# Two-block kernel: second-layer weights, W_out, Wqkv and a fourth weight pair loaded in 32-wide blocks and turned by VectorE

## What is computed

```
xn = layernorm(x)
s0 = xn + rmsnorm(kvec * (xn @ W_in.T) @ W_out.T) * norm_w     # recurrent step from a zero state
ffn = fwht(silu(xn @ W1.T) * (xn @ W3.T)) @ W2.T                # H = 1024
x  = x + s0 * silu(ffn)
xn = layernorm(x);  z = layernorm(xn) * gamma + beta
s1 = softmax(causal(z Wq (z Wk).T / 16)) @ (z Wv) @ Wo + xn
x  = x + s1 * silu(ffn with the second layer's weights)
```

## Time and profile before

| | |
|---|---|
| median of 3 runs | 363.26 us (363.02 to 363.34) |
| profiled execution | 363.3 us, its span 361.5 us |
| PE, PEld, DVE, ACT, POOL busy | 98%, 83%, 69%, 47%, 28% |
| DMA | 38.63 MB in 42336 packets, 34.8% of 16 engines on SP's queue |
| chain that ended last | PE 94%, DMA 3%, DVE 1%, SP queue 1% |

### The profile page before, as it was taken

The page is one execution under the profiler, slowest core; times in us unless marked ns, Lnnn a source line. Parts: engine busy times, 40 slices in busy tenths (PEclk is TensorE's granted clock), DMA queues, the critical chain, the costliest instruction groups (busy, mean ns, idle before and its releaser), DMA issues.

```text
span 361.5 us, 5052 instructions
## 1 busy us (share of the span) xinstructions
PE 355.8 (98%) x1821; PEld 301.5 (83%) x1821; DVE 250.6 (69%) x481; ACT 169.2 (47%) x335; POOL 100.8 (28%) x126
## 2 busy tenths in 40 slices
PE   7999999999999999999999999999999999999996
PEld 4878888888888888888988878888888888888896
DVE  5669965886489647868568894788646887356645
ACT  2865371355135623554275544644446354454510
POOL 2154410246014723467506030060300603004000
PEclk9999999999999999999999999999999999999999
DMA  7995110525145623440242401424204332054001
GB/s 239 287 320 198 60 59 0 176 58 170 35 133 159 190 74 117 120 145 0 72 134 67 141 0 60 151 54 126 81 30 160 74 117 88 0 190 111 20 3 58
DMA packets 42336, 38.63 MB, mean 107 GB/s; under 512 B 5700, under 2 KB 41800, under 8 KB 42312
## 3 DMA queue, kind: packets, MB, share of 16 engines
q1 hardware_dynamic: 42168, 38.25, 34.8%
q10 hardware_dynamic: 144, 0.07, 0.1%
HBM read 24.09 MB, written 14.22 MB: 106 GB/s over the span
## 4 chain that ended last, share of the span: by engine, by line
PE 94%; DMA 3%; DVE 1%; SPq 1%; issue 0%; ACT 0%
PE GU L362 19%; PE GU L363 19%; PE GU L364 19%; PE O L362 8%; PE O L363 8%; PE O L364 8%; DMA stage<-in_L_ffn_W 3%; PE O L369 1%; PE T L369 1%; PE O L433 1%; PE T L362 1%; PE T L364 1%; PE T L363 1%; PE O L519 1%; PE O L518 1%; PE O L517 1%
## 5 line engine op out<-in xcount | busy, mean ns | idle before, releaser
L730 ACT ACTIVATE hf<-GU 128x512 f32<-128x512 f32 x64 | 38.2, 599 | 80.3 <-DVE hid L854 55.8
L1001 DVE TENSOR_TENSOR hf<-hf,GU 128x512 f32<-128x512 f32 x64 | 43.6, 681 | 32.5 <-PE GU L364 27.1
L362 PE MATMUL GU<-XT,W1T 128*128 128x512 f32 x128 | 50.8, 397 | 0.0
L364 PE MATMUL GU<-XT,W1T 128*128 128x512 f32 x128 | 49.9, 390 | 0.0
L363 PE MATMUL GU<-XT,W1T 128*128 128x512 f32 x128 | 49.9, 390 | 0.0
L362 PE MATMUL GU<-XT,W3T 128*128 128x512 f32 x128 | 49.9, 390 | 0.0
L364 PE MATMUL GU<-XT,W3T 128*128 128x512 f32 x128 | 49.8, 389 | 0.0
L363 PE MATMUL GU<-XT,W3T 128*128 128x512 f32 x128 | 49.8, 389 | 0.0
L854 DVE TENSOR_TENSOR hid<-hf,hid 128x512 fp32r<-128x512 f32 x64 | 48.2, 754 | 1.2 <-ACT hid L661 0.8
L362 PE MATMUL O<-hid,W2hi 128*128 128x512 f32 x112 | 44.0, 393 | 0.0
L363 PE MATMUL O<-hid,W2hi 128*128 128x512 f32 x112 | 43.7, 390 | 0.0
(11 more groups left out here) (204 smaller groups left out, 741.2 us busy)
## 6 DMA issues: line engine op xcount, KB each, us to landing
stage<-in_L_ffn_W SPq DMA_DIRECT2D x24, 256.0 KB, 5.6
swap_rows<-GX SPq DMA_DIRECT2D x7, 512.0 KB, 3.6
sT<-swap_rows SPq DMA_DIRECT2D x28, 128.0 KB, 2.7
swap_gate<-GX SPq DMA_DIRECT2D x7, 512.0 KB, 2.9
sT<-swap_gate SPq DMA_DIRECT2D x28, 128.0 KB, 2.7
swap_p<-PX SPq DMA_DIRECT2D x4, 640.0 KB, 3.2
PL<-swap_p SPq DMA_DIRECT2D x16, 160.0 KB, 3.2
swap_w<-GX SPq DMA_DIRECT2D x4, 512.0 KB, 2.9
```

Source lines behind the costliest of these rows:

```text
L362: pe.matmul(o, lhs(0), rhs(0), start=start, stop=False)
L364: return pe.matmul(o, lhs(1), rhs(0), start=False, stop=stop)
L730: act.activation(hf[:, c % 2, :], GU[:, c % 2, 0, :], ACT.Silu).then_inc(silu_done, 1)
L1001: dve.tensor_tensor(hf[:, c % 2, :], hf[:, c % 2, :], GU[:, c % 2, 1, :], ALU.mult).then_inc(mul_done, 1)
```

## The change

Weights that TensorE transposed, or that went over DRAM, are now loaded so that only 32 x 32 blocks are left to turn. `load_blocks` issues four DMAs a matrix; each fills 32 partitions, and each contiguous run that it reads is 32 floats. VectorE turns the blocks in place (`in_place`).

- First layer's fourth pair: W1 and W3 by blocks (8 DMAs), turned by VectorE in front of `nat_lo(3)`, hi by ACT, lo by POOL (`last_hi`, `last_lo`); chunk 6 waits for `last_lo`. W2 as before.
- W_out and Wqkv: by blocks (4 DMAs each) right into `woutT` and `wqkvT`; turned by VectorE (`turn_wout` after chunk 5, `turn_wqkv` after chunk 6).
- Second layer: W1 and W3 by blocks into `stage` (8 DMAs a pair), W2 by blocks into U2 (4 DMAs for all). VectorE turns them in groups 1 and 2, ACT makes hi, POOL makes lo. No `swap_w`, no transposes on TensorE past the head; a Hadamard product behind chunk 7 in groups 1 and 2, and behind chunk 1 in groups 2 and 3.
- The scaling of win by kvec goes from VectorE to ACT. `normalise(1)` comes ahead of `k_vector` and chunk 5.
- X is loaded in three parts; its last 1 MB comes behind Wqkv and Wo.
- All butterflies of the second layer are in groups 2 and 3.

```diff
+            def load_blocks(to, src, done):
+
+                blocks = src.rearrange("(d b) (c q a) -> q b c d a", b=Q, q=QUADS, a=Q)
+                for q in range(QUADS):
+                    sp.dma_start(to[q * Q:(q + 1) * Q].rearrange("b (c d a) -> b c d a", d=D // Q, a=Q), blocks[q]).then_inc(done, 16)
...
-            sp.dma_start(X[:, TILES:, :], xt_dram[:, TILES:, :]).then_inc(xrest_loaded, 16)
+            sp.dma_start(X[:, TILES:2 * TILES, :], xt_dram[:, TILES:2 * TILES, :]).then_inc(xnext_loaded, 16)
...
-            sp.dma_start(wout[:, :, :], W_out.rearrange("(a p) n -> p a n", p=P)).then_inc(small_loaded, 16)
+            load_blocks(woutT[:, :, :].rearrange("p m d -> p (m d)"), W_out, wout_loaded)
             sp.wait_ge(w2_tr, 2)
-            load_pair(0, 3, stage[:, 1, :, :], stage_loaded[1])
+            for w, m in enumerate((W1[0], W3[0])):
+                load_blocks(stage[:, 1, w, :], m[6 * P:8 * P, :], stage_loaded[1][w])
...
-            load_pair(1, 0, stage[:, 0, :, :], stage_loaded[0])
-            sp.wait_ge(w2_tr, PAIRS)
-            load_pair(1, 1, stage[:, 1, :, :], stage_loaded[1])
+            load_w(PAIRS)
             move_rows(1)
+            sp.wait_ge(last_lo, 2)
+            load_w(PAIRS + 1)
+            load_blocks(U2[1][:, :, :].rearrange("p c d -> p (c d)"), W2[1], w2_loaded)
             for n in range(1, NB):
                 move_gate(n - 1)
-                for j in ((0,), (1, 2), (3,))[n - 1]:
-                    move_w(PAIRS + j)
+                if n == 2:
+                    load_w(PAIRS + 3)
                 if n == NB - 1:
                     spread_c2(0)
                 move_rows(n + 1)
-                if n < 3:
-                    sp.wait_ge(w1_lo, 2 * KC * n)
-                    sp.wait_ge(w2_tr, PAIRS + n)
-                    load_pair(1, n + 1, stage[:, (n + 1) % 2, :, :], stage_loaded[(n + 1) % 2])
+                if n == 1:
+                    load_w(PAIRS + 2)
...
@@ TensorE: head and groups
-                head_pair(3)
                 head_pair_w2(3)
...
             def small_m():
-                pe.wait_ge(kstep, KSTEPS)
-                pe.wait_ge(sm_nat, 2)
+                pe.wait_ge(win_scaled, MC)
+                pe.wait_ge(wout_turned, MC // 2)
...
             def block0_group(n):
-                pe.wait_ge(u_ready, PAIRS + (0, 2, 3)[n - 1])
+                pe.wait_ge(u_ready, PAIRS + (0, 1, 3)[n - 1])
...
+                    if c == 1 and n > 1:
                         pe.wait_ge(gateT_ready, 2 * n)
-                        next_pair_w2(PAIRS + (0, 2, 3)[n - 1])
...
+                        next_hadamard(PAIRS + 2 * n - 3)
+                if n < 3:
+                    pe.wait_ge(gateT_ready, 2 * n)
+                    next_hadamard(PAIRS + 2 * n - 2)
                 recurrent_mix(n)
...
@@ VectorE: the head
-                dve.wait_ge(xrest_loaded, 16)
-                pair_lo(0, 3, 3)
+                dve.wait_ge(xnext_loaded, 16)
+                for w in (0, 1):
+                    dve.wait_ge(stage_loaded[1][w], 80)
+                    in_place(stage[:, 1, w, :]).then_inc(last_turned, 1)
                 nat_lo(3, w2nat)
                 stats(1, TILES)
                 chunk(0, 4)
+                normalise(1, TILES)
                 k_vector()
                 chunk(0, 5)
-                normalise(1, TILES)
+                turn_wout()
                 x_turn(1)
                 chunk(0, 6)
+                turn_wqkv()
                 w2_sums(0)
...
@@ POOL: groups 1 to 3
+                if n > 1:
+                    nat_lo(PAIRS + 2 * n - 3)
+                    pair_butterfly(1, 2 * n - 4, PAIRS + 2 * n - 3)
...
+                pool.wait_ge(xn_ready, n + 3)
+                if n < 3:
+                    pair_lo(PAIRS + 2 * n - 2)
+                    nat_lo(PAIRS + 2 * n - 2)
+                if n > 1:
+                    pair_butterfly(1, 2 * n - 3, PAIRS + 2 * n - 2)
+                    quad_butterfly(1, n - 2, (17, 23)[n - 2])
+                if n < 3:
+                    pair_lo(PAIRS + 2 * n - 1)
+                else:
+                    last_butterfly(1, 25)
```

More of the change, by code:

```diff
@@ L164, in two_block_kernel, with landed @@
         xT = [[XT[:, a, k, :] for k in range(KC)] for a in (0, 1)]
[L165 to L177, removed]
+        def landed(i):
+            return (32, 80)[i % 2] + 64 * (i // 2 - 1)
         def blocks_of(a, c0, c1):
@@ L279, in move_p @@
                                  swap_p[j].rearrange("(q a) f -> a q f", q=QUADS)).then_inc(p_moved, 16)
[L281 to L289, removed]
             def spread_c2(m):
@@ L435, in small_m @@
                 last.then_inc(sm_mm, 1)
[L436 to L439, removed]
             def small_av():
-                pe.wait_ge(sm_nat, 5)
+                pe.wait_ge(wqkv_turned, 3)
+                pe.wait_ge(wo_loaded, 16)
                 for i in range(KC):
@@ L467, in up_chunk @@
                     pe.wait_ge(xt_ready, 2 * n + 2)
-                if first and c % 2 == 0:
+                if first and c in (2, 4):
                     pe.wait_ge(w_lo, c + 2)
+                elif first and c == 6:
+                    pe.wait_ge(last_lo, 2)
                 if c >= 2:
@@ L667, in pair_hi, with turned_hi, turned_nat_hi @@
                        w_tr, 2 * i + w + 1, w_hi)
-            def landed_hi(i):
-                act.wait_ge(w_moved, 64 * (i - PAIRS) + 64)
-                for w in (0, 1):
-                    for k in range(KC):
-                        act.activation(w_part(0, i, w, k), w_landed(i, w, k), ACT.Copy).then_inc(w1_hi, 1)
+            def turned_hi(i):
+                cols = bass.ds(2 * P * (i - PAIRS), 2 * P)
+                for w, WT in enumerate((W1T[1], W3T[1])):
+                    hi(WT[:, 0, :, cols], stage[:, i % 2, w, :].rearrange("p (k h) -> p k h", k=KC), w_turned, 2 * (i - PAIRS) + w + 1, wx_hi)
+            def turned_nat_hi(i):
+                j = i - PAIRS
+                act.wait_ge(h_done, i)
+                hi(w2nat[:, 0, :, :], U2[1][:, 2 * j:2 * j + 2, :], w2_turned, j + 1, natx_hi)
             def pair_u(l, i, j):
@@ L759, in block0_head @@
                 pair_u(0, 2, 2)
-                pair_hi(0, 3, 3)
+                for w, WT in enumerate((W1T[0], W3T[0])):
+                    hi(WT[:, 0, :, 6 * P:8 * P], stage[:, 1, w, :].rearrange("p (k h) -> p k h", k=KC), last_turned, w + 1, last_hi)
                 nat_hi(3, w2nat)
@@ L764, in block0_head @@
                 pair_u(0, 3, 3)
-                small_hi([(woutT[:, 2 * h:2 * h + 2, :].rearrange("p a d -> p (a d)"), T[:, h, :]) for h in (0, 1)],
-                         2, sm_tr, 1, sm_nat)
                 hi(gb[:, :, :].rearrange("p g k -> p (g k)"), O[:, 0, 0:2 * KC], gb_tr, 1, gb_ready)
+                act.wait_ge(kvec_ready, 1)
+                for m in range(MC):
+                    act.activation(win[:, m, :], win[:, m, :], ACT.Identity, scale=kvec[:, m:m + 1]).then_inc(win_scaled, 1)
                 chunk(0, 6, True)
                 hi(flat[0], O[:, 0, :], sm_mm, 1, sm_hi)
-                small_hi([(wqkvT[:, w, :, :].rearrange("p a d -> p (a d)"), (T[:, 0, :], T[:, 1, :], O[:, 1, :])[w]) for w in range(3)],
-                         3, sm_tr, 3, sm_nat)
                 w2_hi(0)
@@ L888, in k_vector @@
                 dve.tensor_reduce(kvec[:, :], kprod[:, 0, :, :], AX_X, ALU.add).then_inc(kvec_ready, 1)
-                dve.wait_ge(kvec_ready, 1)
-                for m in range(MC):
-                    dve.tensor_scalar(win[:, m, :], win[:, m, :], kvec[:, m:m + 1], None, ALU.mult).then_inc(kstep, 1)
             def small_lo(q):
```

142 lines of the change are left out of this document (73 added, 69 removed).

## The result

| | before | after |
|---|---|---|
| median | 363.26 us | 366.91 us (366.80 to 367.21, 5 runs) |
| profiled execution, its span | 363.3, 361.5 us | 367.18, 365.4 us |
| ratio to before, 95% interval | | 1.0105 (1.0094 to 1.0116) |

The change costs 3.65 us. I had forecast 360.9, a gain, with 364.5 as the upper end of the range: wrong in sign, and outside the range.

What follows compares the result with a forecast made beforehand. TensorE, busy 98%, was taken as the bound. Gains of 0.72 us (head) and 1.76 us (groups 1 to 3), 2.5 us off 363.3, gave 360.8, forecast as 360.9; its own range 360.2 to 361.8, the full range 359.5 to 364.5.

Steps and rivals of the forecast that it cites:

- Step (1) of the head: Chunk 4 on TensorE, with 4 transposes instead of 12 ahead, starts at 25.0 instead of 26.48 us.
- DMA step: SP's queue: W_out and fourth-pair blocks, at 1030 packets in a us, take 8.0 us, through at 24.5; W3 needed at 25.9.
- third rival: Fourth pair's blocks land late, VectorE waits before its turn; slower than before from 2.5 us late, about 720 packets/us; chance 0.18.
- The rival of the clock: TensorE's clock falls at the new 3.1 us stall ahead of M, which takes up to 3.45 us more; chance 0.10.
- Steps (2) to (4): Head: chunk 6 at 31.05; VectorE's list stalls TensorE 3.1 us, M at 37.05; head ends at 49.66, winning 0.72 us.
- the meeting: Rival: VectorE's normalisation in the head runs beside POOL's butterflies, costing 1.1 us for one tile, 4.5 for four; chance 0.14.
- fourth rival: The rival of the clock: clock drop from 2.4 to 1.2 GHz behind the stall ahead of M, 362.6 to 364.3; chance 0.10.
- By 0.5 us an operation it is done 0.2 us before: Group ends: ACT finishes the second pair 0.2 us before the U copy is needed; otherwise a few tenths in two groups.
- Moving the last butterflies forward costs nothing on TensorE: Second layer: moving its last butterflies forward adds no TensorE time.
- the price of the transposes: TensorE: 0.11 us each, 44 removed, 4.8 us: 3.08 in the head and 1.76 in groups 1 to 3.
- no wait for the turned Wqkv: Head: VectorE's three turns of Wqkv end near 41.2 us, needed at 43.4, so hidden.
- no wait for POOL's late Hadamard input: Group 1: POOL's W2 subtraction ends at 82.2, TensorE wants it after chunk 7 at 83.2; one us to spare, no stall.

Runs made afterwards that it cites:

- k12_fill: Changed kernel with 18 unused 512-column matmuls on TensorE ahead of its wait for W2 of the fourth pair; 364.76 us, 1.0041 of the kernel before.
- k4_pairfirst: Changed kernel with the fourth pair's W2, then its W1 and W3 blocks, loaded ahead of W_out's blocks; 366.37 us, 1.0087 of the kernel before.
- k9_warm: k4_pairfirst plus 15 unused 512-column matmuls on TensorE ahead of the waits of product M; 363.03 us, 0.9993 of the kernel before.
- k8_runs: Changed kernel, W_out and the fourth pair's W1 and W3 read as contiguous runs, same DMAs and bytes, output differs; 365.81 us, 1.0067 of before.
- k7_best: Changed kernel with fourth pair loaded and transposed as before, ACT's U copy first, c2 turned a chunk earlier; 361.05 us, 0.9936 of before.
- k2_ucopy: Changed kernel with ACT's copy of U ahead of the second pair's high halves in groups 1 and 2; 365.44 us, 1.0062 of before.
- k3_c2: Changed kernel with the small turn of c2 one chunk earlier in group 3; 365.64 us, 1.0066 of the kernel before.
- k11_all: k7_best with chunk 7 ahead of the product M on TensorE; 359.83 us, 0.9908 of the kernel before.
- k5_oldpair: Changed kernel with the fourth pair loaded (3 DMAs) and transposed on TensorE as before; 362.26 us, 0.9968 of the kernel before.
- k1_w2first: Changed kernel with W2 of the fourth pair issued ahead of that pair's block loads; 368.32 us, 1.0139 of the kernel before.

## Why the prediction was wrong, point by point

The sum was 360.8 for the profiled execution, and that took 367.18. By stretches: the head +3.57 (53.23 against 49.66), groups 1 to 3 +1.38 (-0.38 instead of -1.76), group 4 +1.45 (nothing forecast): 6.40.

- **Step (1) of the head failed: "chunk 4 starts at 25.0".** It started at 29.75. My own DMA step had W3 through at 24.5, with W2 behind it in the queue; I named that and gave it 0.3 us. W2 landed at 29.1, and TensorE stood for 4.6 us. TensorE needs W2 at 24.5, before it needs W1 or W3, so the deadline of "W3 needed at 25.9, fits by a us" was the wrong one to test.
- **The DMA step was mis-sized.** I had 8192 packets in 8.0 us; SP needed 10.8 us to issue them, 760 in a us, near the 720 from which my third rival turns slower. I took the rate from the row of 64-byte packets and asked how fast engines drain packets. The packets were indeed quick: from 18 to 26 us the 16 engines were busy 77.8% for 840 packets in a us, 14.8 ns each. From 18.8 to 20.8 us they were full, at 980 packets in a us, near my 1030. From 20.8 to 25.5 us, with block loads still being issued, they were busy 60% for 730 in a us: there SP's issue set the pace, and that is the term that my sum lacked. W3 was turned at 27.5, 1.6 us late as priced by that rival; its mechanism was right, its place was not: TensorE's wait for W2, not VectorE's for W3, came last.
- **The rival of the clock came true** (0.10 in the text), behind another stall than named. There it cost about 0.3 us (k12_fill). For a stall ahead of M I had said up to 3.45 us; the runs show 2.9 (k4_pairfirst against k9_warm) and 1.7 (k8_runs, k7_best).
- **Steps (2) to (4) were right where their premise held.** In k4_pairfirst chunk 6 started at 31.02 (31.05), the normalisation took 1.38 us clear of POOL, M came at 37.96 (37.05). What I had missed is POOL's additions on the low half of chunk 5, not on the normalisation: I looked for the meeting at the one row where the trace of before showed it. And the chain that I had forecast held a 3.1 us stall of its own. Had I joined the fourth rival to the forecast, instead of giving it 0.10 beside it, the forecast would have been 360.8 plus what a stall costs in clock: 364.3 by my own price, 362.5 to 363.7 by the measured ones. No gain, or hardly any.
- **"By 0.5 us an operation it is done 0.2 us before" failed.** ACT's copy of U came after its need, by up to 0.9 us in group 2, and cost 1.5 us in all (k2_ucopy). The slow scatter of the gate made it worse: with it TensorE waited up to 0.9 us, in the runs without it 0.4. A cover of 0.2 us at the end of a chain of four rows of 0.5 us was no cover.
- **"Moving the last butterflies forward costs nothing on TensorE"** says nothing of what cost 1.3 us there. That the spread of c2, now issued late, holds up `move_rows` behind it, with TensorE waiting at the end for ZT, wasn't in my list at all (k3_c2).
- **Right:** the price of the transposes; no wait for the turned Wqkv in the changed kernel; no wait for POOL's late Hadamard input. With the stalls taken out they are won: k11_all is 3.4 us below the kernel before, although its fourth pair is transposed on TensorE again. Group 1's -1.10 is less than it looks, as 0.45 us of it is the product that went to group 2.

The losses by the runs: the fourth pair's blocks 4.65 us, U 1.5, c2 1.3, together 7.4 us, beside a net loss of 3.65. Taken away at once they would leave 359.5; k7_best took 361.05, and 360.1 in the three executions without the lower clock. They overlap: in k5_oldpair the waits for U and ZT were already 0.7 us each instead of 1.2. For U that goes with the gate's scatter, 2.9 us there and 4.7 in the changed kernel, and for ZT with the scatter behind the spread, 4.5 us against 5.3. Whether a packet of code falls into a scatter is set by when each comes, and which edit moves that no run shows; so some tenths of each of the three figures may be the other's.

## What to carry to other kernels

A load that is cut into short runs costs time on the queue that issues it: add up the issue times to the first load that anyone waits for, whatever its kind, and put that one ahead. Taking work from a busy engine is only a gain if the next instruction is ready; a stall on TensorE costs its length and, where TensorE sets the pace behind it, 1.7 to 2.9 us in clock on top (stalls of 2.3 and 4.0 us), and moving a ready chunk into the gap avoids most of both. Give a cover that is shorter than one instruction no credit.

## What the hardware showed

- SP's issue of one 64 KB load in 128-byte runs (512 packets): 0.84 us in the head of the changed kernel, 0.665 us in groups 1 and 2 and behind a W2 that itself took 1.88 us (k1_w2first); with long runs 0.57. Of 128 KB (W_out, 1024 packets): 1.0 us first in the row, 0.70 us behind the pair in k4_pairfirst; with long runs 0.48. It does not grow with the count of packets alone.
- The spread of one line over 128 partitions (256 KB) moved at about 90 GB/s and took 4.8 us to land; a scatter of 512 KB issued 1.8 us behind it landed in 5.3 us, 4.3 us behind it in 3.2.
- TensorE's granted clock fell behind waits of 4.6, 4.0 and 2.3 us, and behind two waits of 0.7 and 1.7 us close together (k1_w2first); it did not behind waits of 0.6, 0.9 or 1.2 us. At the lower level the matmuls of 512 columns started 0.43 us apart. Behind the same wait of 3.97 us the lower level lasted to nearly 44 us in k4_pairfirst, and to a little past 42 in k8_runs.
- The 512 KB scatter of group 1's gate took 4.2 to 4.8 us in the seven traces with a packet of the instruction queue in it, and 2.9 us in the six without.
- A tensor_tensor of VectorE on 512 columns, 0.68 us alone, took 1.04 us in the changed kernel, 1.73 in k4_pairfirst and 2.46 in k5_oldpair beside POOL's; between two executions of the same code in the head one row was 1.08 or 1.76 us.
